# A two-layer transformer kernel: gathering and adding the expert rows in batch 3 instead of spread over batches 2 and 3 of the first attention

## The chip, the cores and the metric

The kernel runs on one core of a Trainium2 chip. The metric is the device time of one execution in microseconds (us). "TensorE" is PE in the profile (its weight loads are PEld), "VectorE" is DVE, "ScalarE" is ACT, "GpSimd" is POOL and "SyncE" is SP. SBUF is the on-chip memory that all of them read and write, and PSUM is the eight banks that TensorE writes.

## The reference

The input is x, four sequences ("batches") of 512 tokens with 256 features. Two layers follow each other; each adds an attention branch and a mixture-of-experts branch to x. Only the first layer matters here:

```python
xn = _layernorm(x)
x  = x + _L0_attn_ref(xn, ...) + _L0_ffn_ref(xn, ...)
```

The attention has 16 heads of 128 features. Per head h: q = rope(xn Wq[h]), k = rope(kp * kh[:, h]) and v = vp * kh[:, 16 + h], where kp and vp are shared by all heads and kh holds one number per token and head; then causal scores q k', softmax, p v, and the product with Wout. The expert branch picks, for each token, the 4 best of 32 experts, and adds to x the sum over k of weight[k] * (output row of expert k for this token).

## The kernel before, in words

The program is a list of stages with a barrier between them: norm and routing; attention of batches 0 and 1 (while GpSimd scatters the normalised rows to their experts' slots in DRAM); the experts, which leave their output rows in `ys` in DRAM; attention of batches 2 and 3, called with `extra="combine"`; then the second layer. The change is in this second call of `attention_block0`.

The block treats one head of one batch at a time: 32 heads u = 0 to 31, of which 0 to 15 are batch 2 and 16 to 31 are batch 3. Every engine has its own instruction stream, written out by hand in the order of u; semaphores tie the streams together, and `wait_ge` blocks everything that stands behind it on that engine. The order of work is fixed by these streams alone.

Per head u, and by line:

- ScalarE copies the head's query weights to their high part (`split_high`, L1101), GpSimd subtracts for the low part (`split_low`, L856). Weights of head u+1 are split by GpSimd in its pass u, those of u+3 by ScalarE in its pass u.
- TensorE's pass u: `scores(u)` (L917, L919); then `turn_and_query(u - 1, u + 2)`, which transposes the probabilities of head u-1 (L933) and puts the six query matmuls of head u+2 (L901) between them, the first of them behind a wait for `split_low(u + 2)`; in batch 3 a quarter of an output projection of the batch before (`project_quarter`, L955); then `values(u - 1)` (L949).
- VectorE's pass u: four row maxima (`maxima`, L1025); two weighted rows added to x (`combine`, L1043); rope of head u+2 (L298 to L300); reciprocal (L1033) and four scalings (L1037) of the softmax (`normalise`). In batch 3, one pass in four ends with `add_out` (L1051).
- ScalarE's pass u: exponentials (L1110), copies of the transposed probabilities (L1123) and of the head's output (L1128).
- GpSimd's pass u: the key kT = kp * kh (L867); `split_low(u + 1)` (L856); the query sum qT (L872), which waits for rope; then two indirect DMAs (L878). Each fetches, for 128 tokens, one of their four expert rows from `ys` into one of four places `gath[k]` in SBUF.

There are 16 tiles of 128 tokens and 4 rows per token: 64 gathers and 64 combines, two per head in all 32 passes. `gath` holds the four rows of one tile only. So gather (t, k) waits until combine (t-1, k) has read its place, and combine (t, k) waits until gather (t, k) has landed:

```python
pool.wait_ge(x_added, added_at["row", t - 1, k])   # GpSimd, before gather (t, k)
dve.wait_ge(gathered[k], 16 * (t + 1))             # VectorE, before combine (t, k)
```

With two per pass, a place is used again two passes later.

Of the kernel before, what the change touches and what calls it, by code (L numbers as in the profile page):

```python
# [30 lines left out]
EXPERTS, TOPK = 32, 4  # L31
# [9 lines left out]
H0, D0, I0 = 16, 128, 96  # L41
# [252 lines left out]
def rope0(nc, s, src):  # L294

    h = D0 // 2
    cos, sin = s.c("cos0"), s.c("sin0")
    nc.vector.tensor_tensor(s.rope_a, src[:, :], cos, ALU.mult)  # L298
    nc.vector.tensor_tensor(s.rope_b[h:, :], src[0:h, :], sin[0:h, :], ALU.mult)
    return nc.vector.tensor_tensor(s.rope_b[0:h, :], src[h:, :], sin[h:, :], ALU.mult)  # L300
# [456 lines left out]
def scatter_tile(nc, s, d, layer, t, scattered, choices=range(TOPK)):  # L757

    slot = s.slot_r if layer == 0 else s.slot_w
    for k in choices:  # L760
        nc.gpsimd.indirect_dma_start(  # L761
            out=d["xs"], out_offset=bass.IndirectOffsetOnAxis(ap=slot[:, k, t:t + 1], axis=0),
            in_=s.xn[:, t, :], in_offset=None, bounds_check=SLOTS - 1, oob_is_err=False,
        ).then_inc(scattered[k], 16)
# [29 lines left out]
def attention_block0(nc, s, d, rows, extra):  # L794
    NU = len(rows) * H0
    combining = extra == "combine"
# [4 lines left out]

    added = []
    for u in range(NU):
        if combining:
            added += [("row", u // 2, 2 * (u % 2)), ("row", u // 2, 2 * (u % 2) + 1)]
        if u >= H0 and u % 4 == 3:
            added.append(("out", u // H0 - 1, u % H0 // 4))
    added += [("out", len(rows) - 1, i) for i in range(ROWS)]
    added_at = {x: n + 1 for n, x in enumerate(added)}
# [4 lines left out]
    def added_before(x):  # L814
        n = added_at[x] - 1
        return max([m + 1 for m in range(n) if tile_of(added[m]) == tile_of(x)], default=0)

    with signals(nc, f"a{rows[0]}") as sem, ExitStack() as ctx:
# [4 lines left out]
        wout_done, x_added = map(sem, ("wout_done", "x_added"))  # L823
        w_in = [sem(f"wq_in{i}") for i in range(2)]
        kh_in = [sem(f"kh_in{i}") for i in range(2)]
        gathered = [sem(f"gathered{i}") for i in range(UNROLL)]
# [22 lines left out]
        @block.gpsimd  # L849
        def _(pool):  # L850
            def split_low(u):
                par = u % 2
                pool.wait_ge(whigh, u + 1)
                if u >= 2:
                    pool.wait_ge(q_done, u - 1)
                nc.gpsimd.tensor_tensor(w_parts[1][:, par], s.wq[:, par], w_parts[0][:, par].bitcast(F32),  # L856
                                        ALU.subtract).then_inc(wlow, 1)

            split_low(0)
            split_low(1)  # L860

            for u in range(NU):
                b, par = rows[u // H0], u % 2
                pool.wait_ge(kh_in[par], 16 * (u // 2 + 1))
                if u >= 2:
                    pool.wait_ge(scored, ROWS * (u - 1))
                nc.gpsimd.tensor_tensor(s.kT[:, par], s.kpT[:, b * SEQ:(b + 1) * SEQ], s.khb[:, par],  # L867
                                        ALU.mult).then_inc(k_ready, 1)
                if 1 <= u < NU - 1:
                    split_low(u + 1)  # L870
                pool.wait_ge(rope_part, u + 1)
                nc.gpsimd.tensor_tensor(s.qT[:, par], s.rope_a, s.rope_b, ALU.add).then_inc(q_ready, 1)  # L872
                t = u // 2
                for k in (2 * (u % 2), 2 * (u % 2) + 1):
                    if combining:
                        if t:
                            pool.wait_ge(x_added, added_at["row", t - 1, k])
                        nc.gpsimd.indirect_dma_start(  # L878
                            out=s.gath[0][:, k], out_offset=None, in_=d["ys"],
                            in_offset=bass.IndirectOffsetOnAxis(ap=s.slot_r[:, k, t:t + 1], axis=0),  # L880
                        ).then_inc(gathered[k], 16)
                    else:
                        scatter_tile(nc, s, d, 0, t, gathered, (k,))
            if not combining:
                for k in range(TOPK):
                    pool.wait_ge(gathered[k], 16 * TILES)
# [115 lines left out]
        @block.vector  # L1002
        def _(dve):
            v = nc.vector

            def low_of_x(bi):
                dve.wait_ge(xhigh, bi + 1)
                b = rows[bi]
                v.tensor_tensor(x_low[bi], s.xnT[:, :, b * SEQ:(b + 1) * SEQ], x_high[bi].bitcast(F32),
                                ALU.subtract).then_inc(xlow, 1)  # L1010

            def rotate(u):
                dve.wait_ge(q_done, u + 1)
                if u:
                    dve.wait_ge(q_ready, u)
                rope0(nc, s, s.ps[6]).then_inc(rope_part, 1)

            def maxima(u):
                par = u % 2
                for n, i in enumerate(ORDER0):  # L1020
                    bank, at = SCORE_BANK[i]
                    dve.wait_ge(scored, ROWS * u + SCORED0[i])
                    if n == 0 and u >= 2:
                        dve.wait_ge(exped, ROWS * (u - 1))
                    v.tensor_reduce(s.negmax[:, par, i:i + 1], s.ps[bank][:, at:at + (i + 1) * P], AX.X, ALU.max,  # L1025
                                    negate=True).then_inc(maxed, 1)

            def normalise(u):
                par = u % 2
                dve.wait_ge(exped, ROWS * (u + 1))  # L1030
                if u >= 2:
                    dve.wait_ge(prob_ready, ROWS * (u - 1))
                v.reciprocal(s.rsum[:, par], s.psumrow[:, par]).then_inc(rsum_ready, 1)  # L1033
                dve.wait_ge(rsum_ready, u + 1)
                for i in reversed(range(ROWS)):
                    row = s.probs[:, par, ROW_AT[i]:ROW_AT[i] + (i + 1) * P]
                    v.tensor_scalar(row, row, s.rsum[:, par, i:i + 1], None, ALU.mult).then_inc(prob_ready, 1)  # L1037

            def combine(t, k):
                dve.wait_ge(gathered[k], 16 * (t + 1))  # L1040
                if added_before(("row", t, k)):
                    dve.wait_ge(x_added, added_before(("row", t, k)))
                v.scalar_tensor_tensor(out=s.x[:, t, :], in0=s.gath[0][:, k], scalar=s.weight[:, t, k:k + 1],  # L1043
                                       in1=s.x[:, t, :], op0=ALU.mult, op1=ALU.add).then_inc(x_added, 1)

            def add_out(bi, i, bank):
                t = rows[bi] * ROWS + i
                dve.wait_ge(wout_done, ROWS * bi + i + 1)
                if added_before(("out", bi, i)):
                    dve.wait_ge(x_added, added_before(("out", bi, i)))  # L1050
                v.tensor_tensor(s.x[:, t, :], s.ps[bank][:, 0:EMB], s.x[:, t, :], ALU.add).then_inc(x_added, 1)  # L1051

            def statistics(tiles):
                for t in tiles:
                    v.bn_stats(s.stats[:, t, :], s.x[:, t, :]).then_inc(stat, 1)

            low_of_x(0)
            rotate(0)
            rotate(1)
            for u in range(NU):  # L1060
                maxima(u)
                if combining:
                    for k in (2 * (u % 2), 2 * (u % 2) + 1):
                        combine(u // 2, k)
                if u == 1:
                    for bi in range(1, len(rows)):
                        low_of_x(bi)
                if u + 2 < NU:
                    rotate(u + 2)
                normalise(u)  # L1070
                if u >= H0 and u % 4 == 3:
                    add_out(u // H0 - 1, u % H0 // 4, 5)

            last = len(rows) - 1
            if combining:
                dve.wait_ge(x_added, added_at["out", last, 0] - 1)
                statistics(range(TILES - ROWS))
            for i in range(ROWS):
                add_out(last, i, LAST_BANKS[i])
                if combining and i:  # L1080
                    dve.wait_ge(x_added, added_at["out", last, i - 1])
                    statistics([TILES - ROWS + i - 1])
            if combining:
                dve.wait_ge(x_added, added_at["out", last, ROWS - 1])
                statistics([TILES - 1])
                for t in range(TILES):
                    dve.wait_ge(stat, t + 1)
                    v.bn_aggr(s.meanvar[:, t, :], s.stats[:, t, :]).then_inc(aggr, 1)
# [752 lines left out]
```

## Time and profile before

| | us |
|---|---|
| Median of 3 runs | 1326.83 (1325.98 to 1328.25) |
| Profiled execution, its own time | 1326.87 |
| Its span, first to last instruction | 1325.7 |

The span has 19842 instructions. Busy time and its share of the span:

| Engine | busy us | share |
|---|---|---|
| TensorE matmul | 1098.2 | 83% |
| TensorE weight load | 826.1 | 62% |
| VectorE | 782.9 | 59% |
| ScalarE | 521.8 | 39% |
| GpSimd | 510.9 | 39% |

These shares are averages over stages with different limits. The block in question runs from about 537 us to about 862 us of the span, so its own stretches have to be read: which engine is busy without a gap there, and what ends the wait of the others. In the rows, "[0.77 <-PE bank L901]" means that the engine sat idle 0.77 us before this instruction and that TensorE's instruction of line 901 ended that wait. "x4" merges four instructions of a kind that follow each other; its time is from the first one's start to the last one's end.

### The profile page before, as it was taken

How to read it: one execution, taken by the hardware profiler on the slowest of the kernel's cores; microseconds unless marked ns; L12 is line 12 of the kernel's file. 1: busy time of each engine (PE TensorE's matmuls, PEld its weight loads, DVE VectorE, ACT ScalarE, POOL GpSimd, SP SyncE). 2: the span in 40 equal slices, each digit the busy share in tenths (PEclk: the TensorE clock that was granted, in tenths of full speed). 3: DMA queues.
4: the chain of work that ended last, by engine and by line, in shares of the span. 5: the costliest groups of instructions: out<-in, count | busy, mean ns of one | idle time of the engine just before them, and what ended most of it. 6: DMA issues, size and time to landing. Idle time of an engine off the chain costs nothing. (4 is left out here: it accounts for less than half of the span.)

```text
span 1325.7 us, 19842 instructions
## 1 busy us (share of the span) xinstructions
PE 1098.2 (83%) x5536; PEld 826.1 (62%) x5538; DVE 782.9 (59%) x1925; ACT 521.8 (39%) x1419; POOL 510.9 (39%) x487
## 2 busy tenths in 40 slices
PE   5669999999949999588889999959679979999100
PEld 5436667777838988355557777855357658888100
DVE  4868776665115555599997766257337545545233
ACT  2336665555204444355555565131123324444000
POOL 0657776555000000555665564043634300000575
PEclk9879999999969999799999999979969979999655
DMA  9432232221456555322222221025578235554343
GB/s 358 186 100 84 92 92 77 76 76 49 191 129 181 179 180 164 108 72 76 78 75 68 79 72 34 1 83 230 182 225 279 95 92 164 161 164 155 102 133 106
DMA packets 116214, 167.21 MB, mean 126 GB/s; under 512 B 15136, under 2 KB 88736, under 8 KB 113952
## 3 DMA queue, kind: packets, MB, share of 16 engines
q1 hardware_dynamic: 76464, 107.46, 25.9%
q0 software_dynamic: 12288, 33.57, 7.9%
q10 hardware_dynamic: 27360, 24.92, 5.4%
q8 instruction: 52, 0.85, 0.3%
q14 instruction: 50, 0.41, 0.1%
HBM read 103.11 MB, written 62.78 MB: 125 GB/s over the span
## 5 line engine op out<-in xcount | busy, mean ns | idle before, releaser
L1211 PE MATMUL bank<-big_a,probsT 128*128 x760 | 199.4, 358 | 0.4 <-DVE probsT L1283 0.4
L856 POOL TENSOR_TENSOR parts<-wq,parts 128x256 fp32r<-128x256 f32 x64 | 49.0, 766 | 382.1 <-ACT parts L1101 382.1
L1110 ACT ACTIVATE probs<-bank,negmax 128x256 f32<-128x256 f32 (+3 forms) x256 | 134.7, 536 | 123.1 <-DVE negmax L1025 114.6
L917 PE MATMUL bank<-kT,qT 128*128 128x256 f32 (+3 forms) x512 | 171.7, 457 | 0.0
L933 PE MATMUL bank<-const,probs 128*128 128x128 f32 x640 | 129.7, 276 | 27.7 <-DVE probs L1037 27.6
L949 PE MATMUL bank<-probsT,big_b 128*128 128x512 f32 (+3 forms) x512 | 149.0, 434 | 0.0
L1289 DVE TENSOR_TENSOR work<-work,bank 128x96 f32<-128x96 f32 (+1 forms) x190 | 51.5, 271 | 159.3 <-ACT work L1256 159.3
L1211 PEld LDWEIGHTS bank<-big_a,probsT 128*128 128x128 f32 x760 | 130.7, 193 | 21.1 <-issue 2.1
L1025 DVE TENSOR_REDUCE negmax<-bank 128x1 f32<-128x256 f32 (+3 forms) x256 | 113.6, 486 | 47.1 <-PE bank L919 46.0
L1700 POOL DMA_INDIRECT big_a<-ys_dram,slot_r x64 | 61.6, 963 | 200.5 <-PEq L1683 181.3
L901 PE MATMUL bank<-parts 128*128 128x512 f32 x256 | 116.9, 492 | 19.8 <-POOL parts L856 15.2
L1123 ACT ACTIVATE probsT<-bank,kh 128x512 f32<-128x512 f32 (+3 forms) x256 | 118.1, 527 | 21.0 <-PE bank L933 15.9
L1201 PE MATMUL bank<-const,probs 128*128 128x128 f32 x380 | 104.5, 278 | 21.4 <-DMA probs<-xs_dram 21.4
L949 PEld LDWEIGHTS bank<-probsT,big_b 128*128 128x128 f32 x512 | 85.9, 190 | 51.2 <-issue 23.5
L1037 DVE TENSOR_SCALAR probs<-probs,rsum 128x512 f32<-128x512 f32 (+3 forms) x256 | 116.0, 515 | 2.3
L955 PE MATMUL bank<-big_b,big_a 128*128 128x256 f32 x512 | 116.3, 379 | 0.0
L917 PEld LDWEIGHTS bank<-kT,qT 128*128 128x128 f32 x512 | 83.3, 193 | 47.3 <-issue 36.4
L933 PEld LDWEIGHTS bank<-const,probs 128*128 128x128 f32 x640 | 84.0, 142 | 45.7 <-DVE probs L1037 32.4
L955 PEld LDWEIGHTS bank<-big_b,big_a 128*128 128x128 f32 x512 | 96.7, 190 | 12.7
L1263 ACT ACTIVATE work<-bank 128x256 f32<-128x256 f32 x190 | 72.8, 383 | 71.0 <-PE bank L1229 70.8
L1256 ACT ACTIVATE work<-bank 128x96 f32<-128x96 f32 (+1 forms) x190 | 50.1, 264 | 125.7 <-PE bank L1211 125.7
L761 POOL DMA_INDIRECT xs_dram<-xn,slot_w x64 | 63.2, 987 | 75.3 <-DVE shift L1622 45.0
(208 smaller groups left out, 2022.8 us busy)
## 6 DMA issues: line engine op xcount, KB each, us to landing
probs<-xs_dram SPq DMA_DIRECT2D x190, 128.0 KB
ys_dram<-work ACTq DMA_DIRECT2D x190, 128.0 KB
work<-khT_dram SPq DMA_DIRECT2D x64, 256.0 KB
xs_dram<-big_a SPq DMA_DIRECT2D x12, 1024.0 KB, 19.5
wq<-in_wq SPq DMA_DIRECT2D x64, 128.0 KB
big_a<-in_gu SPq DMA_DIRECT2D x1, 6144.0 KB, 18.3
stack_dram<-parts SPq DMA_DIRECT2D x24, 256.0 KB
xlow<-stack_dram SPq DMA_DIRECT2D x48, 128.0 KB
```

The lines of the kernel that those rows point to most:

```text
L901: mm = nc.tensor.matmul(s.ps[6][:, :], w_parts[wp][:, u % 2, k, :], (x_high, x_low)[xp][bi][:, k, :], start=n == 0, stop=last)
L917: nc.tensor.matmul(s.ps[bank][:, at:at + w], s.qT[:, par, i * P:(i + 1) * P], s.kT[:, par, 0:w], start=True, stop=False)
L933: mm = nc.tensor.transpose(s.ps[bank][:, at + (i - j) * P:at + (i - j + 1) * P], s.probs[:, par, ROW_AT[i] + j * P:ROW_AT[i] + (j + 1) * P ...
L949: mm = nc.tensor.matmul(s.ps[7][:, j * P:], s.vp[:, rows[u // H0] * ROWS + j, :], s.probsT[:, COL_AT[j]:COL_AT[j] + w], start=n == 0, stop ...
L955: mm = nc.tensor.matmul(s.ps[bank][:, 0:EMB], s.oT[bi][:, h, i * P:(i + 1) * P], s.wout[:, h, :], start=h == 0, stop=h == H0 - 1)
L1025: v.tensor_reduce(s.negmax[:, par, i:i + 1], s.ps[bank][:, at:at + (i + 1) * P], AX.X, ALU.max, negate=True).then_inc(maxed, 1)
L1037: v.tensor_scalar(row, row, s.rsum[:, par, i:i + 1], None, ALU.mult).then_inc(prob_ready, 1)
L1110: nc.scalar.activation(s.probs[:, par, ROW_AT[i]:ROW_AT[i] + (i + 1) * P], s.ps[bank][:, at:at + (i + 1) * P], ACT.Exp, bias=s.negmax[:, p ...
L1123: nc.scalar.activation(s.probsT[:, COL_AT[j]:COL_AT[j] + w], s.ps[bank][:, at:at + w], ACT.Copy, scale=s.kh[:, rows[bi] * ROWS + j, H0 + h ...
L1201: mm = nc.tensor.transpose(s.ps[i % 2][:, k * P:(k + 1) * P], rows_in[:, i % UNROLL, k * P:(k + 1) * P], s.c("ident"))
L1211: mm = nc.tensor.matmul(s.ps[2 + i % 2][:, 0:W], rowsT[:, i % 2, k * P:(k + 1) * P], gu[:, k, bass.ds(e * W, W)], start=k == 0, stop=k == ...
L1263: nc.scalar.activation(outs[:, j], s.ps[6 + i % 2][:, 0:EMB], ACT.Copy).then_inc(out_ready, 1)
```

## The change

In passes 0 to 15 (batch 2) GpSimd gathers nothing and VectorE combines nothing. In passes 16 to 31 (batch 3) each pass treats one whole tile, t = u - 16: GpSimd issues its four gathers after qT, and VectorE adds rows 0 and 1 after the maxima and rows 2 and 3 after `normalise`, ahead of `add_out`. The number of gathers and combines stays 64 each, and there is still one place per k, so it is now used again in the next pass.

```diff
     for u in range(NU):
-        if combining:
-            added += [("row", u // 2, 2 * (u % 2)), ("row", u // 2, 2 * (u % 2) + 1)]
+        if combining and u >= H0:
+            added += [("row", u - H0, k) for k in range(TOPK)]
...
+            def gather(t):
+                for k in range(TOPK):
+                    if t:
+                        pool.wait_ge(x_added, added_at["row", t - 1, k])
+                    nc.gpsimd.indirect_dma_start(
+                        out=s.gath[0][:, k], out_offset=None, in_=d["ys"],
+                        in_offset=bass.IndirectOffsetOnAxis(ap=s.slot_r[:, k, t:t + 1], axis=0),
+                    ).then_inc(gathered[k], 16)
...
                 nc.gpsimd.tensor_tensor(s.qT[:, par], s.rope_a, s.rope_b, ALU.add).then_inc(q_ready, 1)
-                t = u // 2
-                for k in (2 * (u % 2), 2 * (u % 2) + 1):
-                    if combining:
-                        if t:
-                            pool.wait_ge(x_added, added_at["row", t - 1, k])
-                        nc.gpsimd.indirect_dma_start(
...
+                elif u >= H0:
+                    gather(u - H0)
...
                 maxima(u)
-                if combining:
-                    for k in (2 * (u % 2), 2 * (u % 2) + 1):
-                        combine(u // 2, k)
+                if combining and u >= H0:
+                    for k in (0, 1):
+                        combine(u - H0, k)
...
                 normalise(u)
+                if combining and u >= H0:
+                    for k in (2, 3):
+                        combine(u - H0, k)
                 if u >= H0 and u % 4 == 3:
                     add_out(u // H0 - 1, u % H0 // 4, 5)
```

GpSimd's stream in batch 3, before:

```order
L872 TENSOR_TENSOR qT<-work 128x512
L878 DMA big_a<-ys_dram,slot_r 128x256 x2
L867 TENSOR_TENSOR kT<-big_b,work 128x512
L856 TENSOR_TENSOR parts<-wq,parts 128x256
L872 TENSOR_TENSOR qT<-work 128x512
```

and in the changed kernel (where the gather is L863, kT is L876 and qT is L881):

```order
L881 TENSOR_TENSOR qT<-work 128x512
L863 DMA big_a<-ys_dram,slot_r 128x256 x4
L876 TENSOR_TENSOR kT<-big_b,work 128x512
L856 TENSOR_TENSOR parts<-wq,parts 128x256
L881 TENSOR_TENSOR qT<-work 128x512
```

Four gathers instead of two now stand ahead of the key and of the low part of the weights (L856), which TensorE's query matmuls wait for.

VectorE's stream in batch 3, before, from one head's maxima to the next head's:

```order
L1025 TENSOR_REDUCE negmax<-bank 128x1 x4
L1043 SCALAR_TENSOR_TENSOR x_res<-big_a,weight,x_res 128x256 x2
L298 TENSOR_TENSOR work<-bank,const 128x512
L299 TENSOR_TENSOR work<-bank,const 64x512
L300 TENSOR_TENSOR work<-bank,const 64x512
L1033 RECIPROCAL rsum<-sumrow 128x4
L1037 TENSOR_SCALAR probs<-probs,rsum 128x512
L1037 TENSOR_SCALAR probs<-probs,rsum 128x384
L1037 TENSOR_SCALAR probs<-probs,rsum 128x256
L1037 TENSOR_SCALAR probs<-probs,rsum 128x128
L1025 TENSOR_REDUCE negmax<-bank 128x1 x4
```

and in the changed kernel (maxima L1027, combine L1045, reciprocal L1035, scalings L1039):

```order
L1027 TENSOR_REDUCE negmax<-bank 128x1 x4
L1045 SCALAR_TENSOR_TENSOR x_res<-big_a,weight,x_res 128x256 x2
L298 TENSOR_TENSOR work<-bank,const 128x512
L299 TENSOR_TENSOR work<-bank,const 64x512
L300 TENSOR_TENSOR work<-bank,const 64x512
L1035 RECIPROCAL rsum<-sumrow 128x4
L1039 TENSOR_SCALAR probs<-probs,rsum 128x512
L1039 TENSOR_SCALAR probs<-probs,rsum 128x384
L1039 TENSOR_SCALAR probs<-probs,rsum 128x256
L1039 TENSOR_SCALAR probs<-probs,rsum 128x128
L1045 SCALAR_TENSOR_TENSOR x_res<-big_a,weight,x_res 128x256 x2
L1027 TENSOR_REDUCE negmax<-bank 128x1 x4
```

Two of the four combines of a pass now stand at its end, behind the scalings.

## Rows read from the trace of the kernel before

**Rows 1.** Busy time in stretches inside batches 0, 2 and 3 (columns: first row).
```profile
core 0: us, PE busy (x) PEld busy (x) DVE busy (x) ACT busy (x) POOL busy (x), PEclk, DMA share, GB/s
135.00:193.00 58.00, 58.00 (x292) 39.83 (x291) 45.69 (x97) 39.48 (x112) 43.18 (x41) 1.00 0.29 92
...
590.00:660.00 70.00, 59.38 (x288) 39.22 (x286) 68.17 (x113) 38.16 (x113) 42.41 (x41) 1.00 0.25 74
700.00:790.00 90.00, 90.00 (x442) 64.75 (x442) 64.18 (x145) 50.95 (x143) 51.79 (x51) 1.00 0.25 74
```

**Rows 2.** Timeline inside batch 2: start us, us, engine, line, operands, count, [idle before <-releaser].
```profile
641.59 2.27 DVE L1043 SCALAR_TENSOR_TENSOR x_res<-big_a,weight,x_res 128x256 f32<-128x256 f32 x2
...
641.67 1.30 POOL L867 TENSOR_TENSOR kT<-big_b,work 128x512 f32<-128x512 f32 x1
...
646.11 2.65 DVE L1037 TENSOR_SCALAR probs<-probs,rsum 128x512 f32<-128x512 f32 x4
...
648.79 1.68 DVE L1025 TENSOR_REDUCE negmax<-bank 128x1 f32<-128x256 f32 x4
...
648.82 0.44 PE L933 MATMUL bank<-const,probs 128*128 128x128 f32 x2 [1.33 <-DVE probs L1037]
```

**Rows 3.** Timeline, VectorE: reciprocals of heads 0, 16 (batches 0, 1), then 0, 16, 29 (here).
```profile
89.73 0.18 DVE L1033 RECIPROCAL rsum<-sumrow 128x4 f32<-128x4 f32 x1
...
207.72 0.18 DVE L1033 RECIPROCAL rsum<-sumrow 128x4 f32<-128x4 f32 x1
...
555.83 0.18 DVE L1033 RECIPROCAL rsum<-sumrow 128x4 f32<-128x4 f32 x1
...
698.72 0.18 DVE L1033 RECIPROCAL rsum<-sumrow 128x4 f32<-128x4 f32 x1
...
814.04 0.18 DVE L1033 RECIPROCAL rsum<-sumrow 128x4 f32<-128x4 f32 x1
```

**Rows 4.** Timeline inside batch 3, about one head (columns as in rows 2).
```profile
760.36 0.18 DVE L1033 RECIPROCAL rsum<-sumrow 128x4 f32<-128x4 f32 x1
760.58 1.27 DVE L1037 TENSOR_SCALAR probs<-probs,rsum 128x512 f32<-128x512 f32 x4
...
763.10 0.73 POOL L856 TENSOR_TENSOR parts<-wq,parts 128x256 fp32r<-128x256 f32 x1 [3.31 <-ACT parts L1101]
...
764.58 0.19 PEld L901 LDWEIGHTS bank<-parts 128*128 128x128 f32 x1
...
765.19 0.99 POOL L878 DMA_INDIRECT big_a<-ys_dram,slot_r  x1
765.34 1.06 DVE L1043 SCALAR_TENSOR_TENSOR x_res<-big_a,weight,x_res 128x256 f32<-128x256 f32 x2
...
766.49 0.95 POOL L878 DMA_INDIRECT big_a<-ys_dram,slot_r  x1 [0.30 <-issue]
...
767.17 0.69 DVE L298 TENSOR_TENSOR work<-bank,const 128x512 f32<-128x512 f32 x1 [0.77 <-PE bank L901]
767.46 1.28 POOL L867 TENSOR_TENSOR kT<-big_b,work 128x512 f32<-128x512 f32 x1
...
769.30 0.18 DVE L1033 RECIPROCAL rsum<-sumrow 128x4 f32<-128x4 f32 x1
...
```

**Rows 5.** Timeline at the start of the block: from GpSimd to TensorE.
```profile
539.93 0.72 POOL L856 TENSOR_TENSOR parts<-wq,parts 128x256 fp32r<-128x256 f32 x1 [212.24 <-ACT parts L1101]
540.72 0.29 PEld L901 LDWEIGHTS bank<-parts 128*128 128x128 f32 x1 [7.57 <-ACT parts L1101]
```

**Rows 6.** The instructions that use slot_r: last row of that view.
```profile
DMA to landing us min/median/max: 2.4/2.7/4.0
```

**Rows 7.** Timeline of TensorE after a wait near the block's start; then busy time and clock.
```profile
559.47 0.69 PE L933 MATMUL bank<-const,probs 128*128 128x128 f32 x2 [3.66 <-DVE probs L1037]
...
563.28 0.47 PE L901 MATMUL bank<-parts 128*128 128x512 f32 x1
...
560.00:566.00 6.00, 6.00 (x25) 4.34 (x25) 5.87 (x9) 3.98 (x13) 2.23 (x2) 0.76 0.26 87
```

More of the change, by code:

```diff
@@ L872, in _ @@
                 nc.gpsimd.tensor_tensor(s.qT[:, par], s.rope_a, s.rope_b, ALU.add).then_inc(q_ready, 1)
-                t = u // 2
-                for k in (2 * (u % 2), 2 * (u % 2) + 1):
-                    if combining:
-                        if t:
-                            pool.wait_ge(x_added, added_at["row", t - 1, k])
-                        nc.gpsimd.indirect_dma_start(
[L879 to L883, printed above, removed]
+                if not combining:
+                    scatter_tile(nc, s, d, 0, u // 2, gathered, (2 * (u % 2), 2 * (u % 2) + 1))
+                elif u >= H0:
+                    gather(u - H0)
             if not combining:
```

## The prediction, made before the changed kernel was run

> **What bounds the kernel now.** I read three views of the block that works on batches 2 and 3. First, busy time by stretch [rows 1]. In batch 2 VectorE is busy 68.17 of 70 us and TensorE only 59.38; in batch 3 TensorE is busy 90.00 of 90 us and VectorE 64.18. So VectorE bounds batch 2 and TensorE bounds batch 3: the VectorE work of the gathered rows costs time in batch 2 and lies in idle time in batch 3. That is what speaks for the change. Second, the timeline of batch 2 [rows 2]: two combines take 2.27 us there against 1.06 us in batch 3 [rows 4], and the four scalings 2.65 against 1.27, because GpSimd's kT and its other sums run over them; and TensorE's transposes wait 1.33 us for the scalings. Third, the timeline of batch 3 [rows 4], for what a chain of waits through GpSimd would cost. All stretches used have clock 1.00, which is 2.4 GHz.
>
> A result within 0.2% (2.7 us) of the time before counts as no change, since the measurement tells no less apart.
>
> **Batch 2 without gathers and combines.** The trace has this case: batches 0 and 1 run through the same code, with two scatter DMAs per head on GpSimd in place of the gathers, and no combine. In batch 0 TensorE is busy 58.00 of 58 us [rows 1]. From the reciprocal of head 0 to that of head 16, batch 0 took 207.72 - 89.73 = 117.99 us and batch 2 took 698.72 - 555.83 = 142.89 us [rows 3]. The gain is **24.9 us**. GpSimd will have even less to do than in batch 0; TensorE is full there, so I count nothing for it. Ahead of head 0's reciprocal a pair of combines leaves VectorE's path too. Uncontended it takes 1.06 us [rows 4]; the other end is 0, if rope then waits for its queries instead. I take 0.5.
>
> **Batch 3 with four of each: VectorE.** Two more combines per head take 1.06 us [rows 4] out of VectorE's idle time, (90.00 - 64.18) / 90.00 of a head period of 769.30 - 760.36 = 8.94 us, or 2.56 us. VectorE alone would not become the bound.
>
> **Batch 3: the wait that the change adds.** The gather of head v+1 into place 2 must wait until combine (v, 2) has read it, and that combine now stands behind `normalise(v)`, at the end of VectorE's pass. Behind this gather GpSimd has, in order: the gather into place 3, kT of v+2, and `split_low(v + 3)`. TensorE needs the last for the query matmuls of v+3; those matmuls feed rope, after which VectorE does `normalise(v + 1)` and combine (v+1, 2). So there is a ring, once around per head, and its length is a floor for the period:
>
> - first query weight load on TensorE to rope on VectorE: 767.17 - 764.58 = 2.59 [rows 4]
> - rope to reciprocal: 769.30 - 767.17 = 2.13 [rows 4]
> - reciprocal to scalings: 760.58 - 760.36 = 0.22; scalings 1.27 [rows 4]
> - first of two combines: half of 1.06 = 0.53 [rows 4]
> - from its end to the start of the waiting gather: no row shows it. 0.30, the gap between two gathers (766.49 - 765.19 - 0.99 = 0.31); between 0.1 and 0.5
> - gather into place 2: 766.49 - 765.19 = 1.30; into place 3, until kT starts: 767.46 - 766.49 = 0.97 [rows 4]
> - kT 1.28, split_low 0.73 [rows 4]
> - GpSimd to TensorE: 540.72 - (539.93 + 0.72) = 0.07 [rows 5]
>
> The sum is 2.59 + 2.13 + 0.22 + 1.27 + 0.53 + 0.30 + 1.30 + 0.97 + 1.28 + 0.73 + 0.07 = **11.39 us**, longer than the 8.94 us of TensorE's own work. TensorE would sit idle some 2.45 us per head, in one gap ahead of the first query matmul.
>
> What does not enter the ring: qT and the gathers into places 0 and 1 follow split_low (qT taken as long as kT, 1.3 us, and 2.3 us) and end before the next combine (v+1, 2), 6.7 us behind the query start. The gathers land 2.7 us after their issue [rows 6], and each combine comes 5 us or more behind. ScalarE's copy of the weights, for which split_low waits 3.31 us now [rows 4], will be done long before. Combines 0 and 1 may meet kT as in batch 2 [rows 2], yet rope waits for TensorE much longer than that.
>
> **How often.** Head 17's gathers are the first with a wait (tile 0 waits for nothing), and they hold up `split_low(19)`; the last held is `split_low(31)`. The ring therefore sets the 13 periods between the reciprocals of heads 16 and 29. Before, these took 814.04 - 698.72 = 115.32 us [rows 3]; now 13 x 11.39 = 148.1. The loss is **32.8 us**. The last two heads have no query matmuls; kT and qT of head 31 then still come before TensorE wants them, and the last pair of combines falls into the wait for the final projections. I count 0 for the end, at most 1.
>
> **The sum.** -24.9 - 0.5 + 32.8 = +7.4 us. The profiled execution took 1326.87 us, the median of the runs is 1326.83, so the two agree. The forecast is 1326.87 + 7.4 = **1334.3 us**.
>
> **Its own bounds.** The ring could be 11.2 (handoff 0.1). It could be 11.9, if a pair of long instructions meet. One such meeting is combine (v+1, 0) against kT. The row shows kT starting 0.08 us behind the combine, taking its usual 1.30 us, and the combines stretched to 2.27 [rows 2]: GpSimd loses nothing, so I add nothing. The Trainium skill ("SBUF — State Buffer", section "SBUF: two separate sides") states that of such a pair the one which starts first holds the shared port for its whole instruction and the other is blocked; by that rule kT would wait out one combine whenever the combine is first. With one combine of 0.53 us for each of 13 rings that would be 6.9 us more, 1341. The row goes against it here. So the likeliest case has 1331 to 1341.
>
> **Rivals.**
>
> *The ring does not bind (faster).* Were gathers 2 and 3 issued without holding kT and split_low up, because the place was free in time, TensorE would keep its 8.94 us: 13 x 8.94 = 116.2 against 115.3, and the result is 1326.9 - 25.4 + 0.9 = 1302. For it speaks that GpSimd idles 3.31 us per head before split_low [rows 4], enough for two more gathers (2.3 to 2.6 us). Against it: the wait is in the code, combine 2 ends 6.7 us behind the query start, and the gathers, kT and split_low need 4.7 us more. It decides at a ring of 8.94; at a ring of (115.32 + 25.4) / 13 = 10.82 us gain and loss cancel. Chance of 1302: 5%. Between, within 0.2% of before, needs a ring 10.6 to 11.03: 7%.
>
> *The clock falls in the new gaps (slower still).* After a wait of 3.66 us TensorE took 563.28 + 0.47 - 559.47 = 4.28 us to the end of the queries, in a stretch whose mean clock is 0.76, that is partly at 1.2 GHz [rows 7]; at full clock it is the 2.59 of the ring and at most 0.44 for the two transposes ahead [rows 2, 4]. After waits of 1.33 us the clock stayed 1.00 [rows 1, 2]. The new gap of 2.45 lies between. A fallen clock would add 1.25 us (4.28 - 3.03) to 2.6 us (the 2.59 doubled) per ring, 16 to 34 us: 1350 to 1368. The Trainium skill ("TensorE: Matmul & The Clock Gate", section "HAM oscillation — how this bites in real kernels") says that gaps between bursts of matmuls bring the clock down again and again; this rule speaks against the change, and rows 7 agree for the longer gap. Since the queries, scores and projections between gaps are 8.94 us of dense work, I give it 6%.
>
> *Batch 2 gains less,* since its first heads start at other times and clocks than those of batch 0: if a third of the 24.9 us stays away, 1342 to 1343. 7%.
>
> **How the numbers follow.** The ring as summed 75%; the four cases above 5, 7, 6 and 7%. The range 1328 to 1343 holds the likeliest case with its bounds, and much of the two nearest ones. Faster by over 0.2%: 0.06. Within 0.2%: 0.08. Slower: 0.86.
>
> **What would show it.** In the profile after: periods of 7.2 to 7.4 us in batch 2 (117.99 / 16 = 7.37) with TensorE full; in batch 3 periods of 11.4 us, TensorE idle about 2.4 us ahead of L901 or L933, released by GpSimd's `parts` L856; GpSimd's third gather waiting for VectorE's x_res. Wrong: periods of 8.94 us in batch 3 (no ring), TensorE's clock below 1.00 there, or a first head to head 16 time in batch 2 clearly over 118 us.

## The result: 1352.1 us against 1326.7, slower, and by more than forecast

The changed kernel takes 1352.13 us (median of 4, 1347.04 to 1353.11), the kernel before 1326.67 us (median of 4). The ratio is 1.018, with a 95% interval of 1.0155 to 1.021. Forecast were 1334.3 us and a range of 1328 to 1343. So the direction was right and the size was not: 25 us lost instead of 7.6. The profiled execution took 1351.84 us, with a span of 1350.6.

The first question is where the loss lies. VectorE's reciprocal, one per head, marks the heads. Its rows in the timeline of the changed kernel for heads 0, 15, 16, 29 and 31:

```profile
556.26 0.18 DVE L1035 RECIPROCAL rsum<-sumrow 128x4 f32<-128x4 f32 x1
...
667.19 0.18 DVE L1035 RECIPROCAL rsum<-sumrow 128x4 f32<-128x4 f32 x1
...
678.44 0.18 DVE L1035 RECIPROCAL rsum<-sumrow 128x4 f32<-128x4 f32 x1
...
839.49 0.18 DVE L1035 RECIPROCAL rsum<-sumrow 128x4 f32<-128x4 f32 x1
...
854.56 0.18 DVE L1035 RECIPROCAL rsum<-sumrow 128x4 f32<-128x4 f32 x1 [1.50 <-ACT probs L1115]
```

Against [rows 3]:

| heads | before | forecast | after |
|---|---|---|---|
| 0 to 16 (batch 2) | 142.89 | 117.99 | 122.18 |
| 16 to 29 (batch 3) | 115.32 | 148.1 | 161.05 |

Batch 2 gained 20.7 us where 24.9 were forecast, and batch 3 lost 45.7 where 32.8 were. Head 0 came 0.43 us later (556.26 against 555.83). From head 29 to head 31 both kernels take 15.07 us (before: 829.11 - 814.04). The balance up to head 31 is +0.43 - 20.71 + 45.73 = +25.45 us, all of the loss of 25.0.

In batch 2 the reciprocals stand 7.21 to 7.22 us apart from head 3 to head 15. Busy time of the changed kernel, for heads 1 to 15 and heads 16 to 29:

```profile
core 0: us, PE busy (x) PEld busy (x) DVE busy (x) ACT busy (x) POOL busy (x), PEclk, DMA share, GB/s
566.10:667.20 101.10, 101.10 (x506) 69.12 (x505) 79.48 (x169) 69.15 (x196) 48.47 (x45) 1.00 0.19 55
678.44:839.49 161.05, 132.37 (x574) 93.65 (x573) 121.27 (x211) 66.44 (x182) 96.84 (x91) 0.92 0.25 72
```

The second row is the one to read against [rows 1]. TensorE was busy 90.00 of 90 us there and is now idle for 29 of 161; and its clock is 0.92, where it was 1.00.

One ring of batch 3 at full clock, from the timeline (columns as in [rows 2]; the gather is L863, the low part still L856, the reciprocal L1035):

```profile
678.44 0.18 DVE L1035 RECIPROCAL rsum<-sumrow 128x4 f32<-128x4 f32 x1
...
679.85 1.07 DVE L1045 SCALAR_TENSOR_TENSOR x_res<-big_a,weight,x_res 128x256 f32<-128x256 f32 x2
...
680.60 1.14 POOL L863 DMA_INDIRECT big_a<-ys_dram,slot_r  x1 [3.66 <-DVE x_res L1045]
...
682.04 0.95 POOL L863 DMA_INDIRECT big_a<-ys_dram,slot_r  x1 [0.30 <-PE bank L921]
...
683.00 1.27 POOL L876 TENSOR_TENSOR kT<-big_b,work 128x512 f32<-128x512 f32 x1
...
683.66 3.06 DVE L1045 SCALAR_TENSOR_TENSOR x_res<-big_a,weight,x_res 128x256 f32<-128x256 f32 x2
...
684.23 0.97 POOL L856 TENSOR_TENSOR parts<-wq,parts 128x256 fp32r<-128x256 f32 x1
...
685.26 0.19 PEld L903 LDWEIGHTS bank<-parts 128*128 128x128 f32 x1 [2.33 <-issue]
...
687.85 0.69 DVE L298 TENSOR_TENSOR work<-bank,const 128x512 f32<-128x512 f32 x1 [1.13 <-PE bank L903]
...
689.98 0.18 DVE L1035 RECIPROCAL rsum<-sumrow 128x4 f32<-128x4 f32 x1
```

Every link of the forecast ring is there. GpSimd stands 3.66 us before the gather at 680.60 and is let go by VectorE's x_res. The second waiting gather, kT and the low part follow without a break; TensorE's first query load had waited 2.33 us for them. From reciprocal to reciprocal it is 11.54 us. The waits in this stretch, by who waited for whom (total, times, longest):

```profile
POOL big_a L863 <- DVE x_res L1045: 52.9, 14, 4.9
...
PEld bank L903 <- issue: 34.1, 28, 2.6
```

"issue" in the second row means that the profile names no releaser; in the ring above, that wait ends 0.06 us after L856.

And one ring in which the clock falls:

```profile
747.42 1.26 POOL L881 TENSOR_TENSOR qT<-work 128x512 f32<-128x512 f32 x1
747.52 0.19 PEld L903 LDWEIGHTS bank<-parts 128*128 128x128 f32 x1 [2.57 <-issue]
...
748.60 0.78 PE L903 MATMUL bank<-parts 128*128 128x512 f32 x1
...
751.54 0.69 DVE L298 TENSOR_TENSOR work<-bank,const 128x512 f32<-128x512 f32 x1 [2.57 <-issue]
```

The low part is done just before 747.52, and TensorE has waited as before. Then a query matmul, 0.47 us at full clock [rows 7], takes 0.78, and rope starts 4.02 us behind the first load instead of 2.59 (687.85 - 685.26). The granted clock behind the two gaps, in the ring at full clock and in this one (columns as in [rows 1]; PEclk is the third figure from the right):

```profile
686.00:688.00 2.00, 2.00 (x13) 1.66 (x12) 0.87 (x2) 1.52 (x4) 1.54 (x3) 1.00 0.51 145
748.60:751.60 3.00, 3.00 (x11) 2.36 (x10) 0.43 (x2) 1.76 (x5) 2.03 (x3) 0.50 0.37 109
```

Of the 13 intervals from head 16 to head 29, five last 11.29 to 11.55 us and eight last 12.37 to 13.14. Read in slices of 1 us, the clock is at 0.50 for some 3 us once in each of the eight long intervals, and never in the five short ones. It falls after TensorE has taken up work again, not in the gap itself.

Last, the passage from head 15 to head 16, 11.25 us instead of 7.21:

```profile
667.07 0.94 POOL L863 DMA_INDIRECT big_a<-ys_dram,slot_r  x1 [0.30 <-issue]
...
667.40 4.72 DVE L1039 TENSOR_SCALAR probs<-probs,rsum 128x512 f32<-128x512 f32 x4
668.02 1.28 POOL L876 TENSOR_TENSOR kT<-big_b,work 128x512 f32<-128x512 f32 x1
...
669.25 0.98 POOL L856 TENSOR_TENSOR parts<-wq,parts 128x256 fp32r<-128x256 f32 x1
670.19 1.25 POOL L881 TENSOR_TENSOR qT<-work 128x512 f32<-128x512 f32 x1
...
672.18 0.44 PE L935 MATMUL bank<-const,probs 128*128 128x128 f32 x2 [2.45 <-DVE probs L1039]
...
676.32 0.69 DVE L298 TENSOR_TENSOR work<-bank,const 128x512 f32<-128x512 f32 x1 [1.50 <-PE bank L903]
```

The fourth gather of tile 0 starts at 667.07. It waits for nothing, but four of them keep GpSimd until 668.0. kT, the low part and qT then run 3.42 us without a break (668.02 to 671.44), over the four scalings. These take 4.72 us; with two scatters ahead, in the first block, such scalings took 1.75. TensorE's transposes wait 2.45 us for them, and rope starts 676.32 - 672.18 = 4.14 us behind the transposes, so the clock fell here too: it is 0.50 in the stretch from 673.50 to 676.50.

### The profile page after: what moved, and what is told of

It reads as the page before. It is cut to its first block and busy times, and to the rows that moved or that the text cites. A ratio compares the mean times of both kernels' runs of the same rounds, so it can differ in the third digit from the quotient of the medians.

```text
span 1350.6 us, 19844 instructions
## 1 busy us (share of the span) xinstructions
PE 1112.9 (82%) x5538; PEld 835.8 (62%) x5538; DVE 781.4 (58%) x1925; ACT 525.4 (39%) x1419; POOL 514.4 (38%) x487
## 5 line engine op out<-in xcount | busy, mean ns | idle before, releaser
L856 POOL TENSOR_TENSOR parts<-wq,parts 128x256 fp32r<-128x256 f32 x64 | 53.8, 841 | 352.3 <-ACT parts L1106 352.3
L903 PE MATMUL bank<-parts 128*128 128x512 f32 x256 | 124.7, 522 | 48.6 <-issue 28.7
L1128 ACT ACTIVATE probsT<-bank,kh 128x512 f32<-128x512 f32 (+3 forms) x256 | 121.2, 526 | 61.3 <-PE bank L935 60.4
L935 PE MATMUL bank<-const,probs 128*128 128x128 f32 x640 | 136.7, 288 | 9.2 <-DVE probs L1039 9.1
L1027 DVE TENSOR_REDUCE negmax<-bank 128x1 f32<-128x256 f32 (+3 forms) x256 | 113.4, 486 | 35.2 <-PE bank L921 33.6
L1206 PE MATMUL bank<-const,probs 128*128 128x128 f32 x380 | 104.6, 278 | 21.0 <-DMA probs<-xs_dram 21.0
L298 DVE TENSOR_TENSOR work<-bank,const 128x512 f32<-128x512 f32 x64 | 44.3, 692 | 108.5 <-PE bank L903 102.9
L1039 DVE TENSOR_SCALAR probs<-probs,rsum 128x512 f32<-128x512 f32 (+3 forms) x256 | 104.0, 471 | 2.3
L935 PEld LDWEIGHTS bank<-const,probs 128*128 128x128 f32 x640 | 86.7, 146 | 25.6 <-DVE probs L1039 10.5
```

The costliest lines, as they stand in the source:

```text
L903: mm = nc.tensor.matmul(s.ps[6][:, :], w_parts[wp][:, u % 2, k, :], (x_high, x_low)[xp][bi][:, k, :], start=n == 0, stop=last)
L935: mm = nc.tensor.transpose(s.ps[bank][:, at + (i - j) * P:at + (i - j + 1) * P], s.probs[:, par, ROW_AT[i] + j * P:ROW_AT[i] + (j + 1) * P ...
L1128: nc.scalar.activation(s.probsT[:, COL_AT[j]:COL_AT[j] + w], s.ps[bank][:, at:at + w], ACT.Copy, scale=s.kh[:, rows[bi] * ROWS + j, H0 + h ...
L1206: mm = nc.tensor.transpose(s.ps[i % 2][:, k * P:(k + 1) * P], rows_in[:, i % UNROLL, k * P:(k + 1) * P], s.c("ident"))
```

## The experiments

The theories when the experiments were planned. **A**: gathers 2 and 3 wait for a combine behind the scalings, which closes a ring of 11.5 us; the gap that it opens lowers TensorE's clock. **B**: four gathers ahead of kT, or GpSimd and VectorE blocking each other, bound batch 3 whatever the waits. **C**: the fallen clock costs nothing. Each time stands beside the kernel before on the same chip: 1325.32 us for the first four kernels, 1326.53 for the others.

### Two places per k: the wait taken away

```diff
-                    if t:
-                        pool.wait_ge(x_added, added_at["row", t - 1, k])
+                    if t >= 2:
+                        pool.wait_ge(x_added, added_at["row", t - 2, k])
-                        out=s.gath[0][:, k], out_offset=None, in_=d["ys"],
+                        out=s.xn[:, TOPK * (t % 2) + k, :], out_offset=None, in_=d["ys"],
-                    ).then_inc(gathered[k], 16)
+                    ).then_inc((gathered, gathered_odd)[t % 2][k], 16)
```

> The changed kernel with two places per k instead of one (8 tiles of rows in xn, which is free in this block, with a semaphore for each), so that a gather waits for the combine of two tiles before. Nothing else moves: all four gathers stay ahead of kT and the low part of the weights. Theory A (the wait of gathers 2 and 3 for a combine behind the scalings closes a ring of 11.5 us per head, and the gap it opens lowers TensorE's clock): the ring is open, 8.94 us per head in batch 3 with TensorE full and clock 1.00, batch 2 as measured, total 1302 to 1306. Theory B (four gathers ahead of kT, or GpSimd and VectorE blocking each other, bound batch 3 whatever the waits): still over 11 us per head, 1340 or more.

Measured: 1313.32 us (ratio 0.991, 0.989 to 0.993). The ring is gone, and the kernel now beats the one before. But behind the first two intervals the heads of batch 3 alternate between about 8.4 and 10.4 to 10.8 us, 9.46 on average ((802.94 - 679.92) / 13), and not 8.94. Both forecasts miss: A is right on the ring and too low by 7 us, and B falls with its 1340, but its four gathers ahead of kT are what is left. The timeline (of an execution of 1317.17 us, 3.9 above the median):

```profile
707.80 0.95 POOL L864 DMA_INDIRECT xn<-ys_dram,slot_r  x1 [0.30 <-issue]
...
708.14 3.47 DVE L1040 TENSOR_SCALAR probs<-probs,rsum 128x512 f32<-128x512 f32 x4
708.77 1.28 POOL L877 TENSOR_TENSOR kT<-big_b,work 128x512 f32<-128x512 f32 x1
...
710.66 0.87 POOL L857 TENSOR_TENSOR parts<-wq,parts 128x256 fp32r<-128x256 f32 x1 [0.60 <-ACT parts L1107]
...
711.48 1.27 POOL L882 TENSOR_TENSOR qT<-work 128x512 f32<-128x512 f32 x1
711.53 2.10 DVE L1046 SCALAR_TENSOR_TENSOR x_res<-xn,weight,x_res 128x256 f32<-128x256 f32 x2
```

The scalings take 3.47 us where kT and the low part run over them, against 1.27 alone [rows 4], and two combines take 2.10 where qT does, against 1.06. Four gathers ahead of kT have pushed it onto the scalings; the passage from head 15 to head 16 still takes 11.09 us. Moving kT as well, further down, puts this reading to the test. GpSimd's kT takes its usual 1.28 us.

### Half of the rows: the gain of batch 2 by itself

```diff
-            added += [("row", u - H0, k) for k in range(TOPK)]
+            added += [("row", (u - H0) // 2, k) for k in (2 * (u % 2), 2 * (u % 2) + 1)]
```

Gathers and combines of the passes follow the same rule, two per pass, all combines behind the maxima.

> Leaves out the expert rows of tiles 8 to 15: none in batch 2, and in batch 3 two gathers and two combines per head as before the change, for tiles 0 to 7 alone. It takes the gain of batch 2 by itself. Theory A: heads 0 to 16 take 118 to 119 us instead of 142.9, batch 3 keeps 8.94 us per head, total 1301.5 to 1303. A rival, that the gain of batch 2 is partly given back later: above 1306.

Measured: 1303.81 us, 21.5 less than before (ratio 0.984, 0.982 to 0.986). Heads 0 to 16 took 674.06 - 557.53 = 116.53 us, and each head from 16 to 29 then 8.94. So batch 2 gained 142.89 - 116.53 = 26.4 us; head 0 came 1.7 us later (557.53 against 555.83) and batch 3 took 0.9 us more. The gain is real and is not given back. 2.3 us of the 26.4 lie in the first interval alone, 8.33 us against 10.66, and it varies by itself: the changed kernel, whose code is the same up to there, took 9.84. The time is 0.8 us above the range of A. The passage from head 15 to head 16 is 7.21 us here, so the 4 us that it cost the changed kernel are not part of batch 2.

### The late combines ahead of the scalings: the ring shortened

```diff
-                normalise(u)
                 if combining and u >= H0:
                     for k in (2, 3):
                         combine(u - H0, k)
+                normalise(u)
```

> The changed kernel with combines 2 and 3 of a pass ahead of normalise instead of behind it; one place per k as before. Theory A: reciprocal and scalings (0.22 + 1.27) leave the ring, 11.54 - 1.49 = 10.05 us per head at full clock; the gap is 1.1 us, too little for the clock to fall; 13 x 10.05 = 131 against 161 measured, total about 1321. If the clock still falls in the shorter gaps, up to 1333. Theory B: unchanged at 1352.

Measured: 1318.26 us (ratio 0.994, 0.993 to 0.996); the 13 intervals are 9.89 to 9.91 us. Forecast from the ring: 10.05. Busy time in a stretch of its batch 3:

```profile
core 0: us, PE busy (x) PEld busy (x) DVE busy (x) ACT busy (x) POOL busy (x), PEclk, DMA share, GB/s
700.00:780.00 80.00, 74.16 (x356) 52.28 (x355) 68.16 (x132) 40.86 (x114) 59.70 (x58) 1.00 0.32 94
```

The clock stays 1.00 in its rings, where the gap is 0.7 us. It still falls once in the passage from head 15 to head 16, which takes 12.47 us. Two combines ahead of the scalings instead of behind them give back more than the change lost (7.1 us below the kernel before, where the changed kernel is 25.5 above), with the same work and the same places.

### TensorE's gap filled: the clock by itself

```diff
             def query_waits(u):
+                if u:
+                    pe.wait_ge(rope_part, u)
+                if combining and u >= H0 + 2:
+                    for _ in range(2):
+                        nc.tensor.matmul(s.ps[6][:, :], s.c("ident"), s.c("cos0"), start=True, stop=True)
                 pe.wait_ge(whigh, u + 1)
...
-                if u:
-                    pe.wait_ge(rope_part, u)
```

> The changed kernel with two matmuls of constants (fp32, 512 columns, some 1.7 us at full clock) put into TensorE's gap ahead of the first query matmul in batch 3; their result is overwritten. The ring stays as it is. Theory A: the clock stays 1.00 in batch 3, each ring 11.54, 13 x 11.54 = 150 against 161, total about 1341. Rival C (the fallen clock costs nothing, since it falls in time that is waited anyway, or the rings of 13 us have another cause): 1352, rings of 13.1 us remain.

Measured: 1341.11 us (1340.80 to 1342.38), as A forecast. Busy time for its heads 1 to 15 and 16 to 29:

```profile
core 0: us, PE busy (x) PEld busy (x) DVE busy (x) ACT busy (x) POOL busy (x), PEclk, DMA share, GB/s
566.10:666.20 100.10, 100.10 (x502) 68.68 (x500) 78.53 (x166) 68.19 (x194) 48.57 (x45) 1.00 0.19 56
679.48:829.43 149.95, 141.60 (x625) 92.75 (x625) 122.46 (x212) 65.59 (x182) 96.85 (x91) 1.00 0.27 77
```

The clock is 1.00 in batch 3, and 13 rings take 829.43 - 679.48 = 149.95 us, 11.53 each. More work on TensorE made the kernel 11 us faster (10, when each is set against the kernel before on its own chip: 25.5 us lost against 15.8). C falls. The changed kernel by itself says the same: its five intervals without a fall of the clock last 11.49 us on average, and 11.53 is what all 13 last here. The two matmuls are not free everywhere: the passage from head 15 to head 16, where the clock falls as before, takes 13.26 us instead of 11.25. This also splits the loss of batch 3: 161.05 - 149.95 = 11.1 us are the clock, and 149.95 - 115.32 = 34.6 us are the ring.

### Tile 0 gathered earlier: the passage to head 16

```diff
-                elif u >= H0:
+                elif u > H0:
                     gather(u - H0)
+                elif u >= H0 - TOPK and u < H0:
+                    gather(0, (u - H0 + TOPK,))
```

> The changed kernel with the four gathers of tile 0, which wait for nothing, moved from GpSimd's pass 16 to passes 12 to 15, one in each. All else as changed. Theory D (the four gathers of pass 16 push kT, the low part of the weights and qT onto VectorE's four scalings, which then take 4.72 instead of 1.7 us and open the first gap): the interval from head 15 to head 16 falls from 11.25 to 7.2 to 8 us, and the time by 3 to 5 us, to 1347 to 1349, with some us of play from where the clock falls. Rival: the interval stays over 10 us, since it is head 16's own four combines that make it.

Measured: 1344.95 us (ratio 1.014, 1.011 to 1.017), 7 us less than the changed kernel. From head 15 to head 16 it is 7.21 us (674.62 - 667.41): 4.0 us gained, as expected. These 4.0 us hold a fall of the clock that no longer comes there. Of the rest, 2.3 us are the 13 rings, 158.7 us instead of 161.05, with seven long ones instead of eight, and what is left lies behind head 31. The time is below the expected range.

### kT ahead of the gathers, one place per k

GpSimd's pass u, with the body of kT moved into a function `key`:

```diff
+            def key(u):
+                b, par = rows[u // H0], u % 2
+                pool.wait_ge(kh_in[par], 16 * (u // 2 + 1))
+                if u >= 2:
+                    pool.wait_ge(scored, ROWS * (u - 1))
+                nc.gpsimd.tensor_tensor(s.kT[:, par], s.kpT[:, b * SEQ:(b + 1) * SEQ], s.khb[:, par],
+                                        ALU.mult).then_inc(k_ready, 1)
...
+                if u == 0 or not combining:
+                    key(u)
...
                 nc.gpsimd.tensor_tensor(s.qT[:, par], s.rope_a, s.rope_b, ALU.add).then_inc(q_ready, 1)
+                if combining and u + 1 < NU:
+                    key(u + 1)
...
                 elif u >= H0:
                     gather(u - H0)
```

> The changed kernel, one place per k, with kT of head u+1 ahead of the gathers of pass u on GpSimd instead of behind them. Theory A: kT (1.27 us) leaves the ring: 11.54 - 1.27 = 10.3 us per head in batch 3, gap 1.3 us, clock 1.00, total about 1324. Theory B (GpSimd's sums over VectorE's scalings and combines bound batch 3): the ring is not what counts, over 11 us.

Measured: 1323.16 us (1319.91 to 1325.64; ratio 0.997, 0.996 to 0.998). The intervals alternate between 10.33 and 10.67 us, 10.5 on average, where taking 1.27 out of the ring gives 10.3. That the time came out at the forecast 1324 is in part luck: the 13 rings took 2.4 us more than 13 x 10.3, and the passage from head 15 to head 16, which the expectation does not name, 8.24 us instead of 11.25.

```profile
core 0: us, PE busy (x) PEld busy (x) DVE busy (x) ACT busy (x) POOL busy (x), PEclk, DMA share, GB/s
700.00:780.00 80.00, 69.38 (x337) 49.03 (x336) 74.21 (x122) 38.83 (x109) 57.45 (x55) 1.00 0.30 86
```

The clock is 1.00 in this stretch too, although TensorE is idle for 10.6 of 80 us, in gaps of 0.9 and 1.7 us by turns.

### Two places and kT first: a version that beats both

Both diffs together.

> Two places per k and kT ahead of the gathers. With two places alone the heads alternate between 8.4 and 10.4 us, with scalings and combines of 3.4 and 2.1 us where kT, the low part and qT of GpSimd run over them. Theory E (kT, pushed onto the scalings by four gathers, costs the 0.6 us per head over TensorE's 8.94): kT now runs before the gathers and over combines 0 and 1, the scalings are free: 8.94 us per head, TensorE full, total about 1302 to 1305. Rival F (four combines of stretched length are too much for VectorE wherever kT stands): 9.3 us or more per head, 1309 or more.

> As the kernel before in this list, with tile 0 gathered in passes 12 to 15. Theory D and E: nothing is late at head 16 either, 7.2 us from head 15 to 16, total 1301 to 1303, the fastest of all. Rival: no difference to the kernel without this.

Measured: 1303.36 us for the first (ratio 0.9825, 0.980 to 0.985) and 1304.22 us for the second (1302.98 to 1304.71). Theory E holds and F falls: from head 19 to head 29 a head takes 8.95 us ((791.02 - 701.55) / 10). In batch 3 of the first:

```profile
core 0: us, PE busy (x) PEld busy (x) DVE busy (x) ACT busy (x) POOL busy (x), PEclk, DMA share, GB/s
700.00:780.00 80.00, 80.00 (x396) 57.77 (x395) 72.79 (x148) 44.90 (x126) 64.17 (x63) 1.00 0.35 101
```

TensorE is busy 80.00 of 80 us, with all 64 combines in batch 3. How kT now lies:

```profile
741.99 1.29 POOL L874 TENSOR_TENSOR kT<-big_b,work 128x512 f32<-128x512 f32 x1
742.32 1.82 DVE L1053 SCALAR_TENSOR_TENSOR x_res<-xn,weight,x_res 128x256 f32<-128x256 f32 x2
743.42 1.00 POOL L864 DMA_INDIRECT xn<-ys_dram,slot_r  x1
...
746.48 1.46 DVE L1047 TENSOR_SCALAR probs<-probs,rsum 128x512 f32<-128x512 f32 x4
```

It runs over combines 0 and 1, which take 1.82 us in time that VectorE has, and the scalings take 1.46. Against two places alone, whose profiled execution took 13.8 us more than this one, the passage to head 16 is 2.85 us shorter and the 13 intervals together 7.3. Gathering tile 0 earlier adds nothing measurable here, as its rival said: it takes the passage to head 16 from 8.24 to 7.25 us, but from head 16 to head 19 this kernel takes 26.78 us and the other 26.25, and the two times do not differ by more than their own runs do.

## Why the prediction was wrong

**Batch 2, -24.9 us: right.** The first block served as the model, and heads 3 to 15 ran at its 7.21 us. With half of the rows, heads 0 to 16 took 116.53 us against 117.99 forecast. The changed kernel, less the passage to head 16, took 122.18 - 4.04 = 118.14.

**Ahead of head 0, -0.5: not seen.** Head 0 came 0.43 us later. Four other kernels with the same code up to there have it at 554.98 to 557.92 us (the order of the combines changed, and two places), so one profile each cannot tell a term of 0.5 us.

**The ring: right as a mechanism, 0.15 us short.** The forecast was 11.39 us, and 11.54 were read. Link by link, against the working: from the end of the first combine to the gather about 0.22 instead of 0.30 (680.60 - 679.85 - 0.53); gather into place 2 until the next 1.44 instead of 1.30; the low part 0.97 instead of 0.73; the others within 0.1. Combines 0 and 1 run beside the low part (683.66, 3.06 us), and that they lengthen it is likely and not shown: it took 0.96 to 0.98 in 12 of the 13 rings, in which the combines start ahead of it, and 0.72 in the one ring in which they started together with it (771.82 and 771.83). The prediction had taken from [rows 2] that GpSimd loses nothing to a combine; kT indeed keeps 1.27, but the low part, which follows at once, does lose 0.24. The rule of the Trainium skill that was set against this row ("SBUF — State Buffer", section "SBUF: two separate sides") is that the one which starts first blocks the other. The prediction's 0.53 for each ring supposed the combine ahead of kT; in all 13 rings kT started first (683.00 against 683.66), and then the rule has the combines wait, which agrees with their 3.06 us instead of 1.06. Over 13 rings the whole error is 2 us.

**The number of rings: right.** Thirteen, heads 16 to 29; the last two intervals together are unchanged, 15.07 us.

**The clock: the step that failed.** "The clock falls in the new gaps" had a chance of 6%, and a price of 16 to 34 us from a fall in every ring. The sum counted nothing for it, and the range left it out. It fell in eight of 13 and cost 11.1 us, measured by filling the gaps. That is 1.4 us for each fall, within the 1.25 to 2.6 that the prediction named: the price was right, and the chance was not. Without these 11.1 us the profiled execution would have come to 1340.7, inside the range. The argument that the 8.94 us of dense work between gaps would keep it up was not drawn from a row, and no row supports it. The rows that bear on it were the wait of 3.66 us with a fall and that of 1.33 without [rows 1, 2, 7], and a new gap of 2.45 between them deserved about even odds. The Trainium skill ("TensorE: Matmul & The Clock Gate", section "HAM oscillation — how this bites in real kernels") says that gaps between bursts of matmuls bring the clock down again and again. The trace agrees for eight of the 13 rings and not for the other five; the waits in that section's example are longer than the gaps here, so it did not settle the odds either.

**The passage to head 16: missing.** The prediction took batch 0 as the model up to head 16, and said of tile 0 only that its gathers wait for nothing. They still occupy GpSimd, and what stands behind them met the scalings. Their meeting opened a gap of 2.45 us on TensorE, and the clock fell behind it. Both together cost 4.0 us, as moving the gathers showed.

**The sum of the misses:** 0.9 (head 0) + 4.2 (heads 0 to 16) + 1.9 (ring) + 11.1 (clock) = 18.1 us. Between the forecast and the profiled execution lie 1351.84 - 1334.3 = 17.5 us; the part behind head 31 was 0.5 us shorter.

**The rival of 1302:** right on the wait, wrong on the number. Without the wait the kernel took 1313, because kT's place behind four gathers costs VectorE its scalings. It needed kT moved as well to reach 1303. That GpSimd's 3.31 us of idle time would take two more gathers was true for GpSimd alone.

## What to carry to other kernels

When work is packed into fewer passes, look at the buffer that it goes through: the same buffers used twice as often can turn a wait that was met two passes early into a ring, and the length of such a ring can be added up from the rows of the trace before. Then ask two things of the new schedule: what the idle gap does to TensorE's clock, and over which VectorE instruction each moved GpSimd instruction now runs. The cheap cures here were a second buffer and the place of one instruction; with both, 1303 us.

## What the runs showed of the hardware

- In the changed kernel TensorE's weight loads wait before each head's query matmuls, every 11.5 us. Behind eight of nine waits of 2.40 to 2.57 us the clock went to 1.2 GHz for some 3 us, and behind none of four waits of 1.52 to 2.36; the mean of the stretch was 0.92. In four kernels (the changed one, two places, late combines first, gap filled) TensorE's single gap of 2.4 us ahead of head 16 brought it down each time. It stayed 1.00 in all 13 rings of the kernels with gaps of 0.7 us and of 0.9 and 1.7 us. Two matmuls of constants in each long gap of the rings kept it at 1.00.
- GpSimd's sums over VectorE's scalings lengthen these by nearly their own time: 3.42 us of kT, low part and qT made scalings of 1.27 us last 4.72.
- In batch 3 of the changed kernel a gather that had to wait takes 1.14 to 1.18 us and the next starts 1.44 to 1.49 us behind it; one that did not takes 0.94 to 1.01, and the next starts 1.25 to 1.32 behind.
